# A two-layer attention kernel over graphs: tile loads of a turn spread over its slots, and q's last projection moved ahead of two value products

## The chip, the cores and the metric

The kernel runs on one core of one Trainium2 chip. The metric is the device time of one execution in microseconds (us), the median of the runs shown. One more execution was profiled, and the rows below are from it.

## What is computed

64 graphs of 256 nodes with 512 features each, and one adjacency matrix (256 x 256) that all graphs share. Two layers, both with a residual and a layer norm ahead:

```
h = max(layernorm(x), 0)
x = x + attention(h, adj; Wq, bq, Wk, bk, Wv, bv)        # 8 heads of 64, masked softmax
h = max(layernorm(x), 0)
rel = adj.T * (q @ k.T) ;  rel = rel / norm(rel, axis=2) # q = h Wq.T, k = h Wk.T
x = x + rel @ v                                          # v = h Wv.T
```

## The kernel before

**Precision.** Every operand of a large product is held as two fp16 halves, a high one (the fp16 rounding) and a low one (what is left). A product takes three matmuls for each part of the contraction (high x high, high x low, low x high: `SPLIT`). So one projection tile is 12 matmuls of 128 x 512 (`product`, L684).

**Unit of work.** Two graphs form a pair: 512 tokens, 4 tiles of 128. There are 32 pairs. For one pair TensorE makes, in layer 0, the projections `q`, `k`, `v` (4 tiles each), 4 groups of scores into the banks S, and 16 products `pv` (two graphs by eight heads) into the bank O; and in layer 1 the products `rv` and `rq` (4 each), `rel` (2) and `out` (4). Layer 1's q and k weights are multiplied once at the start (`setup_rq` makes `wm`), its v weight is transposed (`setup_rv` makes `wvt`). The products other than scores and pv take turns over three PSUM banks `B`; `free_bank` (L696) makes each wait until the one three places earlier has been evacuated. ACT writes the high half, DVE the low half.

**Transpositions.** What a product needs with the other axis on the partitions is turned by a DMA transposition from SBUF to SBUF, issued by SP: the softmax weights (`probs_t` from `halves`, L319, one for each of the 16 units of a pair), the normed input of layer 0 (`h0t`) and of layer 1 (`h1t`, L292, four each), and `rel_t` (L335, two). For a unit the chain is: scores on TensorE, mask and maximum on DVE (L620), exp on ACT (L481), high half on ACT (L489), low half on POOL (L375), transposition by SP (L319), `pv` on TensorE. The step `split` n stands for ACT's high half, POOL's low half and SP's transposition of unit n.

**Order.** Each engine runs a written-out order of steps. TensorE's is `TENSOR_PLAN`; `PLAN` is shared by SP, POOL, ACT and DVE, which each take the steps that they have a part in. A turn has 26 slots, one large product in each (`SLOTS`, with the number of pairs that the product lags behind); in a turn layer 0 of one pair runs beside layer 1 of the pair before, and out's products are those of two pairs before. `other_slot` puts the steps of a slot in order, and `LOADS` hangs the loads of x behind them: `x_in` (for the layer norm of a pair two turns ahead) and `x_res` (for the residual), four tiles of 128 x 512 fp32 each for a pair, issued by SP (L309, L316) in the same queue as the transpositions and the stores of the result (L340). In `LOADS` they stand two to a slot: x_in in slots 1 and 2, x_res in slots 13 and 14.

```
SLOTS = [("v", 0, 0), ("q", 0, 0), ("rel", 1, 2), ...
         ("k", 2, 0), ("rv", 0, 1), ("rv", 1, 1), ("q", 3, 0), ("rv", 2, 1), ...
LOADS = {13: [("x_res", 0, 0), ("x_res", 1, 0)], 14: [("x_res", 2, 0), ("x_res", 3, 0)],
         1: [("x_in", 0, -1), ("x_in", 1, -1)], 2: [("x_in", 2, -1), ("x_in", 3, -1)]}
```

Waits that matter here: `x_res` n of a pair waits until out n of the pair two before is written (L315); the first `residual` on POOL waits for all four x_res tiles (L388); `x_in` n waits until the tile before it in the buffer has been normed (L308); `rv` n waits for the transposition `h1t` n (L791), `pv` n for that of split n (L771). The buffers `halves` and `probs_t` are rings of four.

Of the kernel before, what the change touches and what calls it, by code (L numbers as in the profile page):

```python
# [5 lines left out]
def adjacency_attention_two_layers(  # L6
# [43 lines left out]

    SLOTS = [("v", 0, 0), ("q", 0, 0), ("rel", 1, 2), ("k", 0, 0), ("v", 1, 0), ("v", 2, 0), ("out", 0, 2),
# [11 lines left out]
    BESIDE = {1: [("squares", 0, 2), ("rel_scale", 0, 2)],
              2: [("residual", 2, 1), ("rel_split", 0, 2)],
              4: [("squares", 1, 2), ("rel_scale", 1, 2)],
              5: [("rel_split", 1, 2)],
              8: [("residual", 3, 1)],
# [7 lines left out]
              17: [("residual", 0, 0)],  # L75
              18: [("ln0_apply", 0, -1), ("ln0_split", 0, -1), ("ln0_apply", 1, -1), ("ln0_split", 1, -1)],
              21: [("ln0_apply", 2, -1), ("ln0_split", 2, -1)],
              23: [("residual", 1, 0)],
              24: [("ln0_apply", 3, -1), ("ln0_split", 3, -1)]}
# [3 lines left out]
    def on(at, steps):

        return [(kind, n, slot // PERIOD) for slot, kind, n in steps if slot % PERIOD == at]

    FIRST = [(slot, 2 * j) for j, slot in enumerate(MASKED)]
    SECOND = [(slot + 1, 2 * j + 1) for j, slot in enumerate(MASKED)]
    BY_UNIT = sorted(FIRST + SECOND)
    ENDED = [slot + 1 for slot in MASKED[1::2]]  # L90

    def tensor_slot(at):

        return (on(at, [(slot, "scores", m) for m, slot in enumerate(SCORED)]) + [SLOTS[at]]
                + on(at, [(slot, "pv", n) for n, slot in enumerate(MULTIPLIED)]))

    def other_slot(at):

        steps = on(at, [(slot + 1, "norm", m) for m, slot in enumerate(MULTIPLIED[3::4])])
        kind, n, back = SLOTS[at - 1]  # L100
        before = [(kind, n, back + (at == 0))]
        if kind == "v":
            steps += before
        steps += on(at, [(slot, "mask", n) for slot, n in FIRST])
        if kind != "v":
            steps += before
        steps += on(at, [(slot - 1, "mask", n) for slot, n in SECOND])
        steps += on(at, [(slot + 1, "inverse", m) for m, slot in enumerate(ENDED)])
        steps += BESIDE.get(at, [])
        for slot, n in BY_UNIT:  # L110
            steps += on(at, [(slot, "exp", n), (slot, "split", n)])
        return steps + LOADS.get(at, [])

    TENSOR_PLAN = [step for at in range(PERIOD) for step in tensor_slot(at)]
    PLAN = [step for at in range(PERIOD) for step in other_slot(at)]
    TURNS = PAIRS + 2

    PROJECT = [(kind, n) for kind, n, _ in SLOTS if kind in ("q", "k", "v")]
    RELATE = [(kind, n) for back in (1, 2) for kind, n, b in SLOTS if b == back]
# [7 lines left out]
    def pairs(plan):  # L127

        for turn in range(TURNS):
            for kind, n, back in plan:  # L130
                if kind in ("rv", "rq", "rel") and turn - back == -1 and (kind, n) in SETUP:
                    yield "setup_" + kind, n, turn - back
                elif 0 <= turn - back < PAIRS:
                    yield kind, n, turn - back
# [15 lines left out]
    with ctx:  # L150
# [18 lines left out]
        mask = sb("mask", [P, NT, N])  # L169
# [3 lines left out]
        x_in = sb("x_in", [P, TILES, D])  # L173
# [74 lines left out]
        residual = sem("residual")  # L248
# [8 lines left out]
        rel_scale = sem("rel_scale")  # L257
# [28 lines left out]
        def _(sp):  # L286
# [59 lines left out]
        def _(pool):  # L346
# [53 lines left out]
        def _(act):  # L400
# [56 lines left out]

            for kind, n, p in pairs(PLAN):
                if kind in ("q", "k"):
# [5 lines left out]
                    dst, b = (q_st, bq) if kind == "q" else (k_st, bk)  # L465
# [7 lines left out]
                elif kind == "exp":  # L473
                    m, g, e = unit(n)
# [51 lines left out]
        def _(dve):  # L526
# [72 lines left out]

            for kind, n, p in pairs(PLAN):  # L600
                if kind in ("q", "k"):
                    c = PROJECT.index((kind, n))
                    dve.wait_ge(p_high, NPC * p + c + 1)
                    dst, b = (q_st, bq) if kind == "q" else (k_st, bk)
# [9 lines left out]
                elif kind == "mask":  # L614
# [68 lines left out]
        def _(pe):  # L683
# [46 lines left out]

            for kind, n, p in pairs(TENSOR_PLAN):
                if kind in ("q", "k", "v"):
# [30 lines left out]
                elif kind == "pv":  # L763
                    m, g, e = unit(n)
# [16 lines left out]
                elif kind in ("rq", "rv", "rel", "out"):  # L781
# [18 lines left out]
                    else:  # L800
                        g, i = n // NT, n % NT
# [31 lines left out]
```

## Time and profile before

| | us |
|---|---|
| runs shown, median (lowest to highest) of 3 | 2463.25 (2459.55 to 2465.02) |
| the profiled execution's own time | 2464.18 |
| its span on the core | 2462.4 |
| TensorE busy | 2396.4 (97%) |
| ACT busy | 1686.4 (68%) |
| DVE busy | 1450.8 (59%) |
| POOL busy | 1298.9 (53%) |

Busy time of TensorE is the time in which a matmul is drawn, and a matmul is drawn somewhat longer than until the next can start. The chain that ended last is TensorE for 84% of the span, and the rest is spread over the other engines and the DMAs with at most 4% each. The DMA engines are busy for 64% of the span, nearly all of it with the packets of SP's queue.

### The profile page before, as it was taken

The page shows a single profiled execution, that of the slowest core. Times are in us where ns is not written, and L with a number is a line of the kernel's source. Part 1 is how long each engine was busy: PE and PEld are TensorE (multiplying, and loading weights), DVE is VectorE, ACT ScalarE, POOL GpSimd, SP SyncE. Part 2 cuts the span into 40 slices and gives each one's busy share as a digit, 9 for nine tenths or more (in the row PEclk, how much of TensorE's full clock was granted, in tenths as well). Part 3 has the DMA queues.
Part 4 walks back from the last instruction along what each step waited for, and adds up shares of the span by engine and source line. Part 5 has one row for each costly group of instructions (what it writes and reads, how often), then busy time and mean ns, then how long its engine had stood idle before and what let it go on. Part 6 is the DMA issues. An engine that isn't in the chain of part 4 may idle for free.

```text
span 2462.4 us, 53549 instructions
## 1 busy us (share of the span) xinstructions
PE 2396.4 (97%) x19252; PEld 1301.3 (53%) x19252; DVE 1450.8 (59%) x4435; ACT 1686.4 (68%) x4111; POOL 1298.9 (53%) x1159
## 2 busy tenths in 40 slices
PE   6999999999999999999999999999999999999986
PEld 3455555555555555555555555555555555555543
DVE  5555666555666556666555665555665556666543
ACT  5667777667676677776677766776776776766762
POOL 3555555555555555555555555555555555555541
PEclk9999999999999999999999999999999999999998
DMA  7566666676676566666665766665755666765652
GB/s 207 111 133 135 131 147 138 123 140 130 137 148 129 120 137 129 153 138 130 126 138 129 151 133 126 140 138 126 150 138 123 140 135 132 150 136 120 124 111 65
DMA packets 938841, 329.14 MB, mean 134 GB/s; under 512 B 885968, under 2 KB 886224, under 8 KB 938576
## 3 DMA queue, kind: packets, MB, share of 16 engines
q1 hardware_dynamic: 935744, 322.31, 63.1%
q8 instruction: 153, 2.51, 0.5%
q10 hardware_dynamic: 2832, 3.41, 0.4%
q14 instruction: 112, 0.92, 0.1%
HBM read 73.93 MB, written 33.55 MB: 44 GB/s over the span
## 4 chain that ended last, share of the span: by engine, by line
PE 84%; DMA 4%; DVE 4%; ACT 3%; POOL 3%; issue 2%; SPq 1%; ACTq 0%; DVEq 0%
PE B L686 70%; PE S L759 7%; PE O L686 6%; DMA probs_t<-halves 3%; ACT probs L481 1%; DVE stats L545 1%; POOL halves L375 1%; ACT h L421 1%; POOL v L371 1%; DMA h1t<-h_halves 1%; PE B L716 1%; ACT halves L489 0%; POOL h_halves L361 0%; ACT h_halves L428 0%; DVE masked L620 0%
## 5 line engine op out<-in xcount | busy, mean ns | idle before, releaser
L375 POOL TENSOR_TENSOR halves<-probs,halves 128x512 f16<-128x512 f32 x512 | 596.5, 1167 | 532.8 <-ACT halves L489 532.6
L481 ACT ACTIVATE probs<-masked,neg_max 128x256 f32<-128x256 f32 x1024 | 508.4, 498 | 222.5 <-DVE neg_max L620 221.8
L620 DVE CUSTOM_DVE_ANT_0 masked<-S,mask 128x256 f32<-128x256 f32 x1024 | 386.4, 417 | 129.4 <-PE S L759 129.3
L361 POOL TENSOR_TENSOR h_halves<-h,h_halves 128x512 f16<-128x512 f32 x256 | 295.0, 1158 | 150.4 <-ACT h_halves L428 150.4
L686 PE MATMUL B<-wv,h0t 128*128 128x512 f16 x1536 | 355.0, 381 | 19.4 <-DMA h0t<-h_halves 19.4
L686 PE MATMUL B<-wvt,h1t 128*128 128x512 f16 x1536 | 349.5, 381 | 12.6 <-DMA h1t<-h_halves 12.6
L686 PE MATMUL B<-h0t,wq 128*128 128x512 f16 x1536 | 352.8, 379 | 1.0 <-DVE k_st L605 0.5
L686 PE MATMUL B<-h0t,wk 128*128 128x512 f16 x1536 | 352.5, 379 | 0.0
L686 PE MATMUL B<-h1t,wm 128*128 128x512 f16 x1536 | 346.9, 379 | 0.0
L489 ACT ACTIVATE halves<-probs 128x512 f16<-128x512 f32 x512 | 322.5, 630 | 16.2
L686 PEld LDWEIGHTS O<-v,probs_t 128*128 128x128 f16 x6144 | 247.7, 98 | 143.0 <-DMA probs_t<-halves 23.8
L686 PE MATMUL O<-v,probs_t 128*128 128x64 f16 x6144 | 263.3, 193 | 17.6 <-DMA probs_t<-halves 17.6
L371 POOL TENSOR_TENSOR v<-v_sum,v 128x512 f16<-128x512 f32 x128 | 148.4, 1159 | 180.9 <-ACT v L472 180.8
L686 PEld LDWEIGHTS B<-wvt,h1t 128*128 128x128 f16 x1536 | 142.0, 98 | 182.8 <-issue 22.6
L391 POOL TENSOR_TENSOR x_res<-x_res,attn 128x512 f32<-128x512 f32 x128 | 162.5, 1269 | 143.7 <-DMA x_res<-in_x_dram 120.8
L686 PEld LDWEIGHTS B<-h0t,wq 128*128 128x128 f16 x1536 | 145.4, 98 | 174.6 <-issue 6.8
L686 PEld LDWEIGHTS B<-wv,h0t 128*128 128x128 f16 x1536 | 141.7, 98 | 179.3 <-issue 28.9
L686 PEld LDWEIGHTS B<-h1t,wm 128*128 128x128 f16 x1536 | 146.1, 98 | 166.6
L686 PEld LDWEIGHTS B<-h0t,wk 128*128 128x128 f16 x1536 | 145.8, 98 | 159.5
L472 ACT ACTIVATE v<-v_sum 128x512 f16<-128x512 f32 x128 | 80.6, 630 | 203.9 <-DVE v_sum L612 203.9
L686 PE MATMUL B<-rv,rel_t 128*128 128x512 f16 x768 | 189.9, 385 | 6.4 <-issue 5.7
L759 PE MATMUL S<-k_st,q_st 64*128 64x256 f16 x3072 | 189.9, 270 | 4.3 <-DVE k_st L605 4.3
(70 smaller groups left out, 2941.8 us busy)
## 6 DMA issues: line engine op xcount, KB each, us to landing
x_in<-in_x_dram SPq DMA_DIRECT2D x128, 256.0 KB, 3.2
x_res<-in_x_dram SPq DMA_DIRECT2D x128, 256.0 KB, 3.8
out_dram<-result SPq DMA_DIRECT2D x128, 256.0 KB, 2.5
probs_t<-halves SPq DMA_TRANSPOSE x512, 2.9
h0t<-h_halves SPq DMA_TRANSPOSE x128, 3.2
h1t<-h_halves SPq DMA_TRANSPOSE x128, 3.3
rv<-in_L_gnn_Wv_dram ACTq DMA_DIRECT2D x2, 512.0 KB, 6.0
rq<-in_L_gnn_Wq_dram ACTq DMA_DIRECT2D x2, 512.0 KB, 7.6
```

Of the source, the lines that this page charges most:

```text
L361: nc.gpsimd.tensor_tensor(h_halves[:, n, 1, :], h[:, n % 2, :], h_halves[:, n, 0, :], ALU.subtract).then_inc(h_low[layer], 1)
L371: nc.gpsimd.tensor_tensor(v[:, p % 2, 1, n, :], v_sum[:, n % 2, :], v[:, p % 2, 0, n, :], ALU.subtract).then_inc(v_low, 1)
L375: nc.gpsimd.tensor_tensor(halves[:, n % RING, 1, :], probs[:, n % 2, :, :].rearrange("p t n -> p (t n)"), halves[:, n % RING, 0, :], ALU.s ...
L391: nc.gpsimd.tensor_tensor(cols, cols, attn[:, n % 2, :, :].rearrange("p (t e) d -> p t (e d)", e=2), ALU.add).then_inc(residual, 1)
L421: nc.scalar.activation(h[:, n % 2, :], src[:, n, :], ACT.Relu, scale=rstd[:, layer, n:n + 1], bias=shift[:, layer, n:n + 1]).then_inc(ln_d ...
L472: nc.scalar.activation(v[:, p % 2, 0, n, :], v_sum[:, n % 2, :], ACT.Copy).then_inc(p_high, 1)
L481: ins = nc.scalar.activation(probs[:, n % 2, i, :], masked[:, n % 2, i, :], ACT.Exp, bias=neg_max[:, n % 2, i:i + 1], scale=-1.0, accum_ou ...
L489: nc.scalar.activation(halves[:, n % RING, 0, :], probs[:, n % 2, :, :].rearrange("p t n -> p (t n)"), ACT.Copy).then_inc(halved_high, 1)
L545: ins = nc.vector.bn_stats(stats[:, layer, t, :], src[:, t, :])
L620: ins = nc.vector.tensor_tensor_reduce(out=masked[:, n % 2, i, :], in0=S[n % 4][:, i, :], in1=mask[:, i, :], scale=SCORE, scalar=BIG, op0= ...
L686: ins = nc.tensor.matmul(dst, left(i), right(j), start=(n == 0), stop=(n == len(pairs) - 1))
L759: ins = nc.tensor.matmul(S[2 * g + e][:, i, :], q_st[own, n, hq, col(g * NT + i)], k_st[own, n, hk, col(g, N)], start=(t == 0), stop=(t == ...
```

## The change

The slots of a turn and the lists of steps are replaced by a table that gives each step of a pair a slot counted from the pair's own start, and a place within the slot; `in_order` sorts the steps of all pairs by slot, place and pair. For TensorE this gives the old order but for one product: q 3 stands at slot 15 and rv 0 and rv 1 at 16 and 17, where before rv 0 and rv 1 stood at 15 and 16 and q 3 at 17. The steps of ACT and DVE that evacuate them move along. The loads of x have slots of their own: x_in at slots 1, 3, 4 and 6 of a turn, x_res at 8, 10, 14 and 15. POOL's order stays as it is. Nothing is added or left out. The code of the engines changes in the name of the list only.

```diff
-    SLOTS = [("v", 0, 0), ("q", 0, 0), ("rel", 1, 2), ("k", 0, 0), ("v", 1, 0), ("v", 2, 0), ("out", 0, 2),
...
+    PRODUCT_AT = {("v", 0): 0, ("q", 0): 1, ("k", 0): 3, ("v", 1): 4, ("v", 2): 5, ("v", 3): 7, ("q", 1): 9,
+                  ("k", 1): 10, ("q", 2): 13, ("k", 2): 14, ("q", 3): 15, ("k", 3): 24,
+                  ("rv", 0): 42, ("rv", 1): 43, ("rv", 2): 44, ("rv", 3): 45, ("rq", 0): 46, ("rq", 1): 47,
...
-    LOADS = {13: [("x_res", 0, 0), ("x_res", 1, 0)], 14: [("x_res", 2, 0), ("x_res", 3, 0)],
-             1: [("x_in", 0, -1), ("x_in", 1, -1)], 2: [("x_in", 2, -1), ("x_in", 3, -1)]}
+    LAYER0 = {"x_in": [-25, -23, -22, -20], "ln0_stats": [-14, -14, -13, -13], "ln0_power": [-13],
+              "ln0_scale": [-10], "ln0_apply": [-8, -8, -5, -2], "ln0_split": [-8, -8, -5, -2],
+              "x_res": [8, 10, 14, 15], "residual": [17, 23, 28, 34]}
...
+    def timetable():
+
+        tensor = [(slot, 0, "scores", m) for m, slot in enumerate(SCORED)]
+        tensor += [(slot, 1, kind, n) for (kind, n), slot in PRODUCT_AT.items()]
+        tensor += [(slot, 2, "pv", n) for n, slot in enumerate(MULTIPLIED)]
...
+        for j, slot in enumerate(MASKED):
+            others += [(slot, 2, "mask", 2 * j), (slot, 4, "mask", 2 * j + 1)]
+            others += [(slot + e, 7, kind, 2 * j + e) for e in range(2) for kind in ("exp", "split")]
+        for layer in (LAYER0, LAYER1):
+            for n in range(TILES):
+                others += [(at[n], 8 if kind[0] == "x" else 6, kind, n) for kind, at in layer.items() if n < len(at)]
+        return tensor, others
+
+    def in_order(steps):
+
+        order = []
+        for p in range(-1, PAIRS):
+            for i, (slot, place, kind, n) in enumerate(steps):
+                if p >= 0 and not (p == 0 and slot < 0):
+                    order.append((PERIOD * p + slot, place, p, i, kind, n))
+                elif p < 0 and (kind, n) in SETUP:
+                    order.append((PERIOD * p + slot, place, p, i, "setup_" + kind, n))
+        return [(kind, n, p) for _, _, p, _, kind, n in sorted(order)]
...
+    TENSOR_PLAN, PLAN = [in_order(steps) for steps in timetable()]
...
-            for kind, n, p in pairs(PLAN):
+            for kind, n, p in PLAN:
```

TensorE, a turn in the middle, from the second group of scores on. `B<-h0t,wq` is a tile of q, `B<-h0t,wk` of k, `B<-wvt,h1t` of rv, `O<-v,probs_t` one pv. Before:

```order
L759 MATMUL S<-k_st,q_st 128x256 x24
L686 MATMUL B<-h0t,wq 128x512 x12
L686 MATMUL O<-v,probs_t 128x64 x12
L686 MATMUL B<-h0t,wk 128x512 x12
L686 MATMUL O<-v,probs_t 128x64 x12
L686 MATMUL B<-wvt,h1t 128x512 x24
L686 MATMUL B<-h0t,wq 128x512 x12
L686 MATMUL O<-v,probs_t 128x64 x12
L686 MATMUL B<-wvt,h1t 128x512 x12
```

And with the change:

```order
L729 MATMUL S<-k_st,q_st 128x256 x24
L656 MATMUL B<-h0t,wq 128x512 x12
L656 MATMUL O<-v,probs_t 128x64 x12
L656 MATMUL B<-h0t,wk 128x512 x12
L656 MATMUL O<-v,probs_t 128x64 x12
L656 MATMUL B<-h0t,wq 128x512 x12
L656 MATMUL B<-wvt,h1t 128x512 x24
L656 MATMUL O<-v,probs_t 128x64 x12
L656 MATMUL B<-wvt,h1t 128x512 x12
```

q 3 has moved ahead of rv 0 and rv 1; the pv behind them is pv 4 in both. (The changed file is 30 lines shorter ahead of the engines' code, so its line numbers are 30 less.)

SP's queue in a turn in the middle, from the h1t transpositions to split 7 (`halves` into `probs_t`: splits 4, 5, 6 and 7). Before:

```order
L292 DMA_TRANSPOSE h1t<-h_halves 128x8x128 x4
L340 DMA out_dram<-result 128x512
L319 DMA_TRANSPOSE probs_t<-halves 128x8x128
L316 DMA x_res<-in_x_dram 128x512 x2
L319 DMA_TRANSPOSE probs_t<-halves 128x8x128
L316 DMA x_res<-in_x_dram 128x512 x2
L319 DMA_TRANSPOSE probs_t<-halves 128x8x128 x2
```

With the change, from the second x_res load on:

```order
L286 DMA x_res<-in_x_dram 128x512
L310 DMA out_dram<-result 128x512
L262 DMA_TRANSPOSE h1t<-h_halves 128x8x128 x4
L310 DMA out_dram<-result 128x512
L289 DMA_TRANSPOSE probs_t<-halves 128x8x128 x2
L286 DMA x_res<-in_x_dram 128x512 x2
L289 DMA_TRANSPOSE probs_t<-halves 128x8x128 x2
```

x_res 0 and 1 no longer stand between splits 4 and 5, and x_res 1 stands ahead of the store of out 2 and of h1t; x_res 2 and 3 are still side by side, right behind split 5.

SP's queue around splits 14 and 15 of a pair and 0 of the next. Before:

```order
L309 DMA x_in<-in_x_dram 128x512 x2
L335 DMA_TRANSPOSE rel_t<-rel_halves 128x8x128
L319 DMA_TRANSPOSE probs_t<-halves 128x8x128
L309 DMA x_in<-in_x_dram 128x512 x2
L319 DMA_TRANSPOSE probs_t<-halves 128x8x128
L335 DMA_TRANSPOSE rel_t<-rel_halves 128x8x128
L319 DMA_TRANSPOSE probs_t<-halves 128x8x128
L340 DMA out_dram<-result 128x512
```

With the change, down to the first x_res load:

```order
L279 DMA x_in<-in_x_dram 128x512
L305 DMA_TRANSPOSE rel_t<-rel_halves 128x8x128
L289 DMA_TRANSPOSE probs_t<-halves 128x8x128 x2
L279 DMA x_in<-in_x_dram 128x512 x2
L305 DMA_TRANSPOSE rel_t<-rel_halves 128x8x128
L289 DMA_TRANSPOSE probs_t<-halves 128x8x128
L279 DMA x_in<-in_x_dram 128x512
L310 DMA out_dram<-result 128x512
L289 DMA_TRANSPOSE probs_t<-halves 128x8x128
L286 DMA x_res<-in_x_dram 128x512
```

Splits 14 and 15 now stand together with one load ahead of them instead of two and two; x_in 3 has moved behind split 0 of the next pair, and x_res 0 of that pair behind its split 1.

## Rows read from the trace of the kernel before

**Rows 1.** Stretch 138 to 2365: length, TensorE busy, granted clock, DMA share, GB/s.
```profile
138.00:2365.00 2227.00, 2215.99 (x17969) 1.00 0.66 135
```

**Rows 2.** TensorE's waits from 130 to 2350: total us, times, longest.
```profile
PE O L686 <- DMA probs_t<-halves: 8.9, 11, 2.1
PE B L686 <- DMA h1t<-h_halves: 2.1, 2, 1.3
```

**Rows 3.** Timeline, first S group of turns 2, 30 and 31: start, length.
```profile
171.57 1.48 PE L759 MATMUL S<-k_st,q_st 64*128 64x256 f16 x24
...
2255.03 1.48 PE L759 MATMUL S<-k_st,q_st 64*128 64x256 f16 x24
...
2328.96 1.48 PE L759 MATMUL S<-k_st,q_st 64*128 64x256 f16 x24
```

**Rows 4.** Timeline, TensorE waits before pv 5, rv 0, pv 15, pv 5, pv 14.
```profile
503.21 0.52 PE L686 MATMUL O<-v,probs_t 128*128 128x64 f16 x12 [1.17 <-DMA probs_t<-halves]
...
715.85 4.48 PE L686 MATMUL B<-wvt,h1t 128*128 128x512 f16 x20 [1.32 <-DMA h1t<-h_halves]
...
846.22 0.52 PE L686 MATMUL O<-v,probs_t 128*128 128x64 f16 x12 [1.77 <-DMA probs_t<-halves]
...
1175.94 0.52 PE L686 MATMUL O<-v,probs_t 128*128 128x64 f16 x12 [2.08 <-DMA probs_t<-halves]
...
1439.27 0.52 PE L686 MATMUL O<-v,probs_t 128*128 128x64 f16 x12 [0.49 <-DMA probs_t<-halves]
```

**Rows 5.** Timeline of turn 13, h1t to pv 5; SPq is SP issuing.
```profile
1011.52 6.13 SPq L292 DMA_TRANSPOSE h1t<-h_halves  x4
...
1014.92 5.34 PE L686 MATMUL B<-wvt,h1t 128*128 128x512 f16 x24
...
1018.32 1.31 SPq L319 DMA_TRANSPOSE probs_t<-halves  x1
1018.33 1.16 POOL L375 TENSOR_TENSOR halves<-probs,halves 128x512 f16<-128x512 f32 x1 [0.61 <-ACT halves L489]
...
1019.68 1.05 SPq L316 DMA_DIRECT2D x_res<-in_x_dram  x2
...
1020.10 2.75 PE L686 MATMUL B<-h0t,wq 128*128 128x512 f16 x12
...
1020.77 1.24 SPq L319 DMA_TRANSPOSE probs_t<-halves  x1
...
1022.05 1.06 SPq L316 DMA_DIRECT2D x_res<-in_x_dram  x2
...
1025.63 0.51 PE L686 MATMUL O<-v,probs_t 128*128 128x64 f16 x12
```

**Rows 6.** The page, DMA issues: count, median us from issue to landing.
```profile
probs_t<-halves SPq DMA_TRANSPOSE x512, 2.9
...
h1t<-h_halves SPq DMA_TRANSPOSE x128, 3.3
```

**Rows 7.** Landing, split 5 in turns 0, 13, 15, 31; last row: split 4, turn 13.
```profile
DMA to landing us min/median/max: 3.7/3.7/3.7
...
DMA to landing us min/median/max: 3.9/3.9/3.9
...
DMA to landing us min/median/max: 7.4/7.4/7.4
...
DMA to landing us min/median/max: 3.8/3.8/3.8
...
DMA to landing us min/median/max: 2.8/2.8/2.8
```

**Rows 8.** Timeline of the start: q 3 and pv 5 of turn 0, rv 0 of turn 1.
```profile
55.33 2.76 PE L686 MATMUL B<-h0t,wq 128*128 128x512 f16 x12 [0.54 <-DVE k_st L605]
...
59.76 0.52 PE L686 MATMUL O<-v,probs_t 128*128 128x64 f16 x12 [0.85 <-DMA probs_t<-halves]
...
119.57 0.81 PE L686 MATMUL B<-wvt,h1t 128*128 128x512 f16 x3 [0.98 <-DMA h1t<-h_halves]
```

More of the change, by code:

```diff
@@ L48, in adjacency_attention_two_layers @@
     RING = 4
-    SLOTS = [("v", 0, 0), ("q", 0, 0), ("rel", 1, 2), ("k", 0, 0), ("v", 1, 0), ("v", 2, 0), ("out", 0, 2),
[3 rows of a table removed]
-    PERIOD = len(SLOTS)
+    PERIOD = 26
+    PRODUCT_AT = {("v", 0): 0, ("q", 0): 1, ("k", 0): 3, ("v", 1): 4, ("v", 2): 5, ("v", 3): 7, ("q", 1): 9,
[3 rows of a table added]
+                  ("out", 0): 58, ("out", 1): 60, ("out", 2): 63, ("out", 3): 64}
+    PROJECT = [(kind, n) for kind, n in PRODUCT_AT if kind in ("q", "k", "v")]
+    RELATE = [(kind, n) for kind, n in PRODUCT_AT if kind in ("rv", "rq", "rel", "out")]
     SCORED = [6, 13, 19, 26]
@@ L61, in adjacency_attention_two_layers @@
     MULTIPLIED = [10, 11, 13, 14, 17, 18, 20, 21, 23, 24, 26, 27, 29, 30, 31, 32]
[L63 to L67, printed above, removed]
[7 rows of a table removed]
[L75 to L79, printed above, removed]
@@ L80, in adjacency_attention_two_layers @@
-    LOADS = {13: [("x_res", 0, 0), ("x_res", 1, 0)], 14: [("x_res", 2, 0), ("x_res", 3, 0)],
-             1: [("x_in", 0, -1), ("x_in", 1, -1)], 2: [("x_in", 2, -1), ("x_in", 3, -1)]}
[L83 to L119, printed above, removed]
+    LAYER0 = {"x_in": [-25, -23, -22, -20], "ln0_stats": [-14, -14, -13, -13], "ln0_power": [-13],
+              "ln0_scale": [-10], "ln0_apply": [-8, -8, -5, -2], "ln0_split": [-8, -8, -5, -2],
+              "x_res": [8, 10, 14, 15], "residual": [17, 23, 28, 34]}
@@ new lines, in adjacency_attention_two_layers @@
+    LAYER1 = {"ln1_stats": [35, 35, 36, 36], "ln1_power": [36], "ln1_scale": [38], "ln1_apply": [38] * TILES,
+              "ln1_split": [38] * TILES, "squares": [53, 56], "rel_scale": [53, 56], "rel_split": [54, 57]}
+    def timetable():
+        tensor = [(slot, 0, "scores", m) for m, slot in enumerate(SCORED)]
+        tensor += [(slot, 1, kind, n) for (kind, n), slot in PRODUCT_AT.items()]
+        tensor += [(slot, 2, "pv", n) for n, slot in enumerate(MULTIPLIED)]
+        others = [(slot + 1, 0, "norm", m) for m, slot in enumerate(MULTIPLIED[3::4])]
+        others += [(slot + 1, 1 if kind == "v" else 3, kind, n) for (kind, n), slot in PRODUCT_AT.items()]
+        others += [(slot + 2, 5, "inverse", m) for m, slot in enumerate(MASKED[1::2])]
+        for j, slot in enumerate(MASKED):
[5 more added lines that the diff above has]
+        return tensor, others
@@ L125, in adjacency_attention_two_layers @@
     NSETUP = len(SETUP)
[L127 to L134, printed above, removed]
+    TENSOR_PLAN, PLAN = [in_order(steps) for steps in timetable()]
     KINDS = ("q", "k", "v", "rv", "rq", "rel", "out", "setup_rv", "setup_rq", "setup_rel")
-    PRODUCTS = [step for step in pairs(TENSOR_PLAN) if step[0] in KINDS]
+    PRODUCTS = [step for step in TENSOR_PLAN if step[0] in KINDS]
     BANKS = 3
@@ L366, in _ @@
                 h_low_half(0, n, 0)
-            for kind, n, p in pairs(PLAN):
+            for kind, n, p in PLAN:
                 if kind == "v":
@@ L456, in setup_high_half @@
                     nc.scalar.activation(dst, bank_[:, :], ACT.Copy, scale=WS).then_inc(setup_high, 1)
-            for kind, n, p in pairs(PLAN):
+            for kind, n, p in PLAN:
                 if kind in ("q", "k"):
@@ L598, in setup_low_half @@
                                                    ALU.mult, ALU.subtract).then_inc(setup_done, 1)
-            for kind, n, p in pairs(PLAN):
+            for kind, n, p in PLAN:
                 if kind in ("q", "k"):
@@ L729, in setup_chunk @@
                 ins.then_inc(setup_product, 1)
-            for kind, n, p in pairs(TENSOR_PLAN):
+            for kind, n, p in TENSOR_PLAN:
                 if kind in ("q", "k", "v"):
```

11 rows, old and new, of tables (BESIDE, PRODUCT_AT, SLOTS) are left out of this document.

## The prediction

> **What bounds the kernel now.** I read the page's busy times first, and TensorE alone is near the span (2396.4 of 2462.4 us). Between 138 and 2365 us it is busy 2215.99 of 2227.00 us at a granted clock of 1.00 (the 2.4 GHz level) [rows 1]. Only TensorE's waits can pay in that stretch, and they are few: 13 shown waits, 11.0 us in all, every one on the landing of a DMA transposition, `probs_t` (11) or `h1t` (2) [rows 2].
>
> To see what lies beyond the shown waits I took the start of the first S group of a turn [rows 3]. From turn 30 to 31 it is 73.93 us, the shortest distance and that of a dozen turns. From turn 2 to 31 it is 2157.39 us for 29 turns, where 29 x 73.93 would be 2143.97: **13.4 us are lost**. The shown waits of these turns make 10.5 (0.54 of the 11.0 fall just ahead of turn 2). The rest is hidden by the modelled ends: a group of 24 is drawn until 1020.26 while the next starts at 1020.10 [rows 5], so each wait is drawn 0.16 us too short (12 x 0.16 = 1.9). 1.0 us is left in waits too short to show. TensorE's own work stays, so this pot and a few waits of the start are all that the change can win.
>
> Where do the 13 waits stand? Before pv 5 (between rv 2 and scores 2): four, 4.5 us, 2.08 and 1.17 the longest. Before pv 15 (between out 0 and v 3): three, 2.6 us, the longest 1.77. Before pv 14: four, 1.9 us, one of 0.49 shown. Before rv 0: two, 2.1 us, the longest 1.32 [rows 4]. These are exactly the places that the change touches.
>
> Then the queue on SP in a turn without a long wait, turn 13 [rows 5]. POOL ends the low half of split 5 at 18.33 + 1.16 = 1019.49. Its transposition is issued at 1020.77, after split 4's own issue (1018.32 to 1019.63) and the two x_res loads (1019.68, two in 1.05 us). It lands 3.9 us later [rows 7], at 1024.67; pv 5 starts at 1025.63. So it has 0.96 us of slack. Transpositions in general land after 2.9 us, this one after 3.7 to 7.4: 3.7 in turn 0, 3.8 in turn 31, median 4.2 of its 32 [rows 6, 7]. The 7.4 is turn 15, and there pv 5 waits 2.08 us [rows 4]. Split 15 is alike: x_in 2 and 3 stand right ahead of it. rv 0 has another reason: the h1t transposition of tile 0 is issued at 1011.52 and lands after 3.3, at 1014.8, and rv 0 starts at 1014.92 [rows 5, 6]. It has 0.1 us of slack in every turn.
>
> **The change part by part.**
>
> *q 3 ahead of rv 0.* It adds no instruction. rv 0 moves back by one product: 1014.92 to 1020.10 are two, so 2.59 us [rows 5]. Its slack becomes 0.1 + 2.6 = 2.7 us, and the longest wait there, 1.32, is gone. I count the two waits (2.1 + 2 x 0.16 = 2.4) and 0.8 of the 1.0 us of small ones, since it is the only place with 0.1 us of slack: **-3.2**. What could be late instead: the bank. Banks go round by three, so the product at each place still waits for the one three places earlier, and that one is evacuated at the same place of ACT's and DVE's programs as before (q 3 now stands where rv 0 stood). rv 3 and rq 0, which now need the banks of rv 0 and rv 1, have a pv and a scores group between. Zero. The wait of q 3 before (k's scores of the pair before) is long past. Zero.
>
> *x_res 0 and 1 no longer between split 4 and split 5.* Split 5 is issued when split 4's issue ends, 1019.65, instead of 1020.77 here; over the turns the distance of 2.44 would mostly fall to 1.8, where POOL is ready, so 0.65 us sooner. And no load is ahead of it in its queue: landing 2.8 to 2.9 instead of 4.2, 1.3 us sooner. Slack 0.96 + 2.0 = 3.0 us. All four waits go: 4.5 + 4 x 0.16 = **-5.1**. The lower bound is the issue alone with the landing unchanged: of the 2.08 then 1.4 stay, of the 1.17 still 0.5, and with the hidden parts about 2.5 of the 5.1 are won.
>
> *x_in 2 and 3 no longer between split 14 and split 15.* The same by 1.1 us of issue (two loads' worth, as the 1.05 us above) and about 1 of landing. The three waits: 2.6 + 3 x 0.16 = **-3.1**; lower bound 2 (1.77 less 1.1 stays).
>
> *x_in 1 no longer ahead of rel's transposition and split 14.* One load of 256 KB less in the queue, the issue of split 14 is unchanged since rel's transposition waits for DVE. Between nothing and all of 1.9 + 4 x 0.16 = 2.5; I take the middle, **-1.25**, as no row decides.
>
> *The start.* q 3 of turn 0 waited 0.54 us for k 2's bank, since two short setup groups stood between; in the new order it needs k 1's bank, long free, and the setup group that needs k 2's comes 2.6 us later. pv 5 of turn 0 waited 0.85 behind the same x_res pair, rv 0 of the first turn 0.98 [rows 8]. With 3 x 0.16: **-2.85**. Lower bound 1.
>
> *What it costs.* Three single loads now stand ahead of other transpositions: x_in 3 ahead of split 1, x_res 0 ahead of split 2, x_res 1 ahead of h1t. By the timeline these land 3.2, 5.9 and (with q 3 moved) 2.7 us before they are needed, and one load costs 0.6 us of issue. x_in 1 and 2 stand ahead of the second rel transposition, which has some 8 us. No wait is added: x_res n needs only out n of two turns earlier, which stands ahead of it on SP. POOL is idle until the x_res loads land in each turn, and they are issued 1 us sooner, which only helps pv 7. I put down **+1.0** for landings that are late by chance at the new places; ends 0 and 3.
>
> Sum: -3.2 - 5.1 - 3.1 - 1.25 - 2.85 + 1.0 = -14.5. The profiled execution took 2464.18 us (span 2462.4), 0.9 above the median of the three runs, 2463.25. 2464.18 - 14.5 = 2449.7; I forecast **2449.5**, as what is won are mostly waits that vary from run to run (2459.55 to 2465.02) and what is left hardly does.
>
> **A rule weighed.** Split 4's transposition has the x_res pair right behind it and lands after 2.8 us in turn 13 as in the median turn; split 5's, with a pair ahead and a pair behind, after 3.9 [rows 5, 7]. I read this as: what is ahead costs, what is behind doesn't. The Trainium skill, "DMA: Bandwidth & Descriptors", section on queues, rings and completion order, says that a later descriptor may finish its write before an earlier one, and that completion is not first in, first out for one issuing engine. By it a pair behind could hurt as well, and in the changed kernel x_res 2 and 3 still stand right behind split 5. The sum would be that of the first rival, 2453.
>
> **The rivals.**
> 1. *Loads behind a transposition hurt as much.* Then pv 5 and pv 15 win the issue time alone (2.5 of 5.1, 2 of 3.1): 2449.5 + 3.7 = 2453.2. For it: the 7.4 of turn 15 has loads on both sides. Against: split 4. Chance 0.15.
> 2. *Late landings are chance and fall elsewhere.* Half of the waits before pv 5 and pv 15 stay (4.1) and all before pv 14 (1.25): 2449.5 + 5.4 = 2454.9. For it: landings of 4.4 to 5.0 us occur here and there at nearly every place of a turn. Against: landings over 5.5 us are found in steady turns only beside load pairs. Chance 0.15.
> 3. *The transposition isn't what is late, the low half ahead of it is*, so moving loads does nothing, or the change doesn't do what it says: x_res 2 and 3 and x_in 1 and 2 are still pairs on SP. Only rv 0 (3.2) and its first wait (1.1) are won: 2459.9, no change. Against: split 5's low half is ready 1.28 us before its issue. Chance 0.09.
> 4. *Slower: h1t behind x_res 1.* x_res 1 now goes out just before out 2's store and the four h1t transpositions. Its place is rv 0, in all 31 turns; the slack there is 2.7 over a landing of 3.3, so it begins to cost at 6.0 us and eats the whole gain at 6.0 + 14.5/31 = 6.5. At 7.4 us each turn [rows 7] it costs 1.4 x 31 = 43: 2493. For it: 7.4 was seen with two loads around. Against: it is one load, issued 2 us before h1t is ready. Chance 0.03.
>
> **How the numbers follow.** The forecast has 0.58. A measurement of this kernel can tell 0.2% from no change, 4.9 us, so faster means below 2458.3. Forecast and rivals 1 and 2 lie there: 0.88 faster; rival 3: 0.09 same; rival 4: 0.03 slower. The range: below, all of the pot with nothing new and half more from pv 14, 2446.5; above, rival 2 with two more microseconds of chance, 2457.5. Outside are rivals 3 and 4 and a little of the rest.
>
> **What the changed profile would show.** A turn of 73.9 us nearly everywhere (over 73.93 by less than 0.15 on average, now 0.46); shown steady waits of some 2 us instead of 11; none before rv 0 except in the last turn (9.5 us there, where no q 3 exists); split 5 issued 1.8 us after split 4 and landing after 2.8. The waits of the last turn, after 2390 us, unchanged. It would be wrong if split 5 still landed after 4 us or more, if waits for `h1t` grew, or if waits appeared before pv 1 or pv 2.

## The result, and the profile after

| | before | changed |
|---|---|---|
| median of 6 runs (lowest to highest), us | 2462.39 (2459.55 to 2465.02) | 2453.95 (2452.83 to 2455.27) |
| the profiled execution's own time | 2464.18 | 2453.71 |
| its span | 2462.4 | 2451.9 |
| start of the first S group of turn 0 | 35.36 | 35.17 |
| turn 0 / turn 1 | 62.25 / 73.96 | 63.90 / 73.47 |
| turns 2 to 30, over 29 x 73.93 | 13.4 | 2.1 |
| from the first S group of turn 31 to the end | 133.4 | 133.3 |

The ratio is 0.996, with a 95% interval from 0.995 to 0.997: the kernel became faster, by 8.4 us of the medians and 10.5 us of the profiled executions. The time lies inside the range that was stated, 4.5 us above the forecast. The table says where the two differ from the plan: the turns in the middle gave 11.4 us, where 11.65 were forecast, and turn 0, which was to give time too, took 1.65 us more.

The page of the changed kernel, busy times, and the windows view of its middle (length, TensorE busy, granted clock, DMA share, GB/s):

```profile
PE 2395.6 (98%) x19252; PEld 1302.3 (53%) x19252; DVE 1442.2 (59%) x4435; ACT 1686.0 (69%) x4111; POOL 1300.1 (53%) x1159
```

```profile
138.00:2355.00 2217.00, 2215.78 (x17988) 1.00 0.66 136
```

Where 11.0 us were idle in 2227 [rows 1], it is now 1.2 in 2217. TensorE's waits from 130 to 2340 us of the changed kernel, the answer to [rows 2]:

```profile
PE O L656 <- DMA probs_t<-halves: 1.0, 4, 0.5
PE B L656 <- DVE q_st L575: 0.2, 1, 0.2
```

No wait for `h1t` is left, and none stands before pv 5 or pv 15. The four for `probs_t` stand before pv 14 (three) and pv 1 (one). The first S groups of turns 2, 30 and 31, the answer to [rows 3]:

```profile
172.54 1.48 PE L729 MATMUL S<-k_st,q_st 64*128 64x256 f16 x24
...
2244.64 1.48 PE L729 MATMUL S<-k_st,q_st 64*128 64x256 f16 x24
...
2318.57 1.48 PE L729 MATMUL S<-k_st,q_st 64*128 64x256 f16 x24
```

A clean turn is 73.93 us as before; 2318.57 - 172.54 = 2146.03 is 2.06 over 29 of them. The timeline of turn 13, from h1t to split 5, the answer to [rows 5]:

```profile
1006.91 5.85 SPq L262 DMA_TRANSPOSE h1t<-h_halves  x4
...
1010.25 2.75 PE L656 MATMUL B<-h0t,wq 128*128 128x512 f16 x12
...
1012.84 5.35 PE L656 MATMUL B<-wvt,h1t 128*128 128x512 f16 x24
1013.43 2.70 SPq L289 DMA_TRANSPOSE probs_t<-halves  x2
1013.72 1.16 POOL L345 TENSOR_TENSOR halves<-probs,halves 128x512 f16<-128x512 f32 x1 [0.61 <-ACT halves L459]
```

q 3 starts where rv 0 started, and rv 0 2.59 us later. Splits 4 and 5 go out one behind the other. Split 5 is issued at 1014.90, as POOL ends its low half, and lands after

```profile
DMA to landing us min/median/max: 2.8/2.8/2.8
```

that is at 1017.7, 3.3 us before pv 5 (1020.97), where it had 0.96. Over all turns from 2 on split 5 is issued 1.7 us after split 4 instead of 2.44.

And the start, TensorE from 56 to 64 us, which answers to the first two of [rows 8]:

```profile
56.11 1.04 PE L692 MATMUL B<-ident,rv 128*128 128x128 f32 x8
...
57.84 0.66 PE L692 MATMUL B<-ident,rv 128*128 128x128 f32 x4 [0.34 <-DVE q_st L575]
58.33 0.51 PE L656 MATMUL O<-v,probs_t 128*128 128x64 f16 x12
58.77 1.48 PE L729 MATMUL S<-k_st,q_st 64*128 64x256 f16 x24
62.88 0.66 PE L692 MATMUL B<-ident,rv 128*128 128x128 f32 x4 [2.62 <-DVE wvt L567]
```

pv 5 of turn 0 no longer waits, but setup_rv 3 now waits 2.62 us until DVE has evacuated the bank of setup_rv 0. In the kernel before it didn't wait.

### The profile page after: what moved, and what is told of

Same layout as the page of the kernel before. It is cut to its first block, busy times and chain, and to the rows that moved or that the text cites. A ratio compares the mean times of both kernels' runs of the same rounds, so it can differ in the third digit from the quotient of the medians.

```text
span 2451.9 us, 53549 instructions
## 1 busy us (share of the span) xinstructions
PE 2395.6 (98%) x19252; PEld 1302.3 (53%) x19252; DVE 1442.2 (59%) x4435; ACT 1686.0 (69%) x4111; POOL 1300.1 (53%) x1159
## 3 DMA queue, kind: packets, MB, share of 16 engines
HBM read 73.93 MB, written 33.55 MB: 44 GB/s over the span
## 4 chain that ended last, share of the span: by engine, by line
PE 93%; DVE 2%; ACT 2%; DMA 1%; issue 1%; POOL 1%; ACTq 0%; DVEq 0%; SPq 0%
PE B L656 78%; PE S L729 7%; PE O L656 7%; DMA probs_t<-halves 1%; ACT probs L451 1%; PE B L686 1%; DVE stats L515 0%; ACT h L391 0%; ACT halves L459 0%; POOL v L341 0%; DVE masked L590 0%; POOL halves L345 0%; ACT h_halves L398 0%; ACTq L377 0%; POOL sq_pow L366 0%
```

## The experiments

They ran on three chips, and the kernel before took a different time on each (medians 2470.07, 2464.29 and 2466.41 us; 2462.39 above). Kernels of one chip are compared with each other, and turns and landings are read from each kernel's profiled execution. The waits by place are taken from the starts of TensorE's rows in turns 2 to 30 (what a step's distance from the one ahead is over its usual distance), hidden parts included:

| turns 2 to 30, us over the usual distance | rv 0 | pv 5 | pv 14 | pv 15 | pv 1 | sum | turn 0, us |
|---|---|---|---|---|---|---|---|
| before | 2.9 | 5.4 | 1.9 | 3.2 | - | 13.4 | 62.25 |
| changed | 0.3 | - | 1.4 | - | 0.5 | 2.1 | 63.90 |
| q 3 alone | - | 5.4 | 1.8 | 4.8 | - | 12.1 | 62.46 |
| loads alone | 9.8 | - | 2.7 | - | 1.4 | 14.1 | 61.52 |
| changed, start as before | 0.4 | - | 2.1 | - | 1.4 | 3.9 | 61.52 |
| before, narrow x_res loads | 2.2 | - | 1.4 | 6.8 | - | 10.2 | 62.40 |

### q 3 alone

```diff
-             ("k", 2, 0), ("rv", 0, 1), ("rv", 1, 1), ("q", 3, 0), ("rv", 2, 1), ("rv", 3, 1), ("rq", 0, 1),
+             ("k", 2, 0), ("q", 3, 0), ("rv", 0, 1), ("rv", 1, 1), ("rv", 2, 1), ("rv", 3, 1), ("rq", 0, 1),
```

> The kernel before with q 3 ahead of rv 0 and rv 1 alone; the loads stay in pairs. My theory: in turns 2 to 31 the waits before rv 0 go (3.2 us), those before pv 5, pv 14 and pv 15 stay (8 to 10 us), and turn 0 loses 2.6 us to a wait of setup_rv 3 for the bank of setup_rv 0, less what pv 5 and q 3 of turn 0 gave up: the turn is 1 to 2 us longer than before. Together 2 to 3 us less than before, ratio 0.999. Rival (the start's loss comes from the loads): turn 0 is not longer, 4 us less.

Measured: 2468.43 us against 2470.07, ratio 0.9993 (0.9984 to 1.0002): no difference that can be told. TensorE's waits from 130 to 2345 us:

```profile
PE O L686 <- DMA probs_t<-halves: 9.0, 13, 2.4
```

The waits for h1t are gone and those for probs_t are all there, as expected. Turn 0 is 0.2 us longer, not 1 to 2: the 2.6 us wait did not come, so it is not q 3's move alone that makes it. Whether the loads alone make it, the next run answers.

### The loads alone

```diff
-                  ("k", 1): 10, ("q", 2): 13, ("k", 2): 14, ("q", 3): 15, ("k", 3): 24,
-                  ("rv", 0): 42, ("rv", 1): 43, ("rv", 2): 44, ("rv", 3): 45, ("rq", 0): 46, ("rq", 1): 47,
+                  ("k", 1): 10, ("q", 2): 13, ("k", 2): 14, ("q", 3): 17, ("k", 3): 24,
+                  ("rv", 0): 41, ("rv", 1): 42, ("rv", 2): 44, ("rv", 3): 45, ("rq", 0): 46, ("rq", 1): 47,
```

> The changed kernel with q 3 back behind rv 1 and rv 0 and rv 1 one slot earlier: the loads' new slots alone. My theory: 8 to 9 us won in turns 2 to 31 (split 5 lands after 2.9 us and is issued 1.8 after split 4), the waits before rv 0 come back (about 3 us in turns 2 to 31), turn 0 keeps the 62 us of before or less, no wait of setup_rv 3: 9 us less than before, ratio 0.996, the same total as the changed kernel by another way. Rival (late landings are chance): the waits before pv 5 and pv 15 are found again in part, 5 us less.

Measured: 2463.38 against 2470.07, ratio 0.9974 (0.9965 to 0.9983): faster by 6.7 us. The execution that was profiled (2465.21) is the slowest of the ten. TensorE's waits from 130 to 2350 us:

```profile
PE B L656 <- DMA h1t<-h_halves: 6.4, 6, 1.6
PE O L656 <- DMA probs_t<-halves: 3.1, 6, 0.9
```

The loads did what was expected at pv 5 and pv 15, but the waits before rv 0 did not come back at 3 us: they are 9.8, in 20 of the 29 turns (2.9 in the kernel before, 2.2 in the kernel with narrow loads, on this chip). x_res 1 now stands ahead of the h1t transpositions, and the one of tile 0 lands after 3.4 us at the median instead of 3.2, with five over 4 instead of two. Where rv 0 has 0.1 us of slack, each of these is a wait. With x_res 1 behind split 5 instead (the run with four loads there) the landing is 3.2 again. So **the two halves of the change help each other**: the new place of x_res 1 costs some 7 us at rv 0 in this execution, and q 3 ahead of it gives the 2.6 us that hide this. By the medians of this chip the loads give 6.7 us, q 3 gives 1.6, and both together (the next kernel) 16.0. Turn 0 is 61.52: the loads alone don't make its wait either.

### The changed kernel with the start as before

```diff
             for i, (slot, place, kind, n) in enumerate(steps):
+                if p == 0 and (kind, n) == ("q", 3):
+                    slot += 2
+                if p < 0 and (kind, n) in (("rv", 0), ("rv", 1)):
+                    slot -= 1
```

> The changed kernel, but in turn 0 q 3 behind the first two setup groups as before. My theory: the 2.6 us wait of setup_rv 3 goes, turn 0 takes about 61.5 us instead of 63.9, all else as in the changed kernel: 2 to 3 us less than the changed kernel, ratio 0.9955 to before. Rival: the time is only moved to the next wait for a landing in turn 0, nothing won.

Measured: 2454.05 against 2470.07, ratio 0.9937 (0.9925 to 0.9949). Turn 0 takes 61.52 us, 2.38 less than in the changed kernel, and the wait is gone. The middle lost 3.9 us in this execution and 2.1 in that of the changed kernel, and the stretch from turn 31 on took 1.2 us more, so the two spans are the same (2452.5 and 2451.9): what the middle loses differs by some 2 us from one execution to the next. On this one chip the step from the loads alone to this kernel, which is q 3's move from turn 1 on, is 9.3 us (2463.38 to 2454.05), where q 3 alone gave 1.6 that can't be told from nothing.

### The kernel before with narrow x_res loads

```diff
-                    sp.dma_start(x_res[:, p % 2, n, :], xv[p][:, n, :]).then_inc(res_loaded[p % 2], 16)
+                    c = D if p < 2 else 16
+                    sp.dma_start(x_res[:, p % 2, n, :c], xv[p][:, n, :c]).then_inc(res_loaded[p % 2], 16)
```

> The kernel before, order untouched, but from pair 2 on each x_res load brings 16 of the 512 columns (so the residual of these pairs is added to what lies there). It takes the bytes ahead of and behind split 5 away and leaves the issues. If the bytes in the queue make split 5 late, it lands after 2.8 to 2.9 us at an unchanged 2.44 us behind split 4, and no wait stands before pv 5 after turn 2: 4 to 5 us less. If the issues are the cause, its landing and the waits before pv 5 stay. The waits before pv 15 and rv 0 stay in both cases.

The kernel leaves out 496 of the 512 columns of each x_res tile from pair 2 on.

Measured: 2464.27 against 2470.07, ratio 0.9977 (0.9967 to 0.9988). SP's queue from 1015 to 1020 us has the same issues, 2.44 us from split 4 to split 5, as before:

```profile
1015.28 1.31 SPq L320 DMA_TRANSPOSE probs_t<-halves  x1
1016.63 1.05 SPq L317 DMA_DIRECT2D x_res<-in_x_dram  x2
1017.72 1.24 SPq L320 DMA_TRANSPOSE probs_t<-halves  x1
1019.00 1.04 SPq L317 DMA_DIRECT2D x_res<-in_x_dram  x2
```

But split 5 lands after 2.8 us at the median (4.2 before), and no wait is left before pv 5. The bytes in the queue made it late, the issues did not (ahead of it or behind, this run doesn't tell; the one with four loads behind does). pv 15, beside the untouched x_in pair, kept its waits (6.8 us in this execution).

### The changed kernel again, on the second chip

> The changed kernel once more, on the chip of the next three, so that they can be set against it. Turns 2 to 31 lose 2 to 4 us, turn 0 takes 63.9 us with a wait of 2.6 for setup_rv 0's bank; three small instructions of DVE's layer norm scale (L507, L509, L534) take 1.1 to 1.2 us each in turn 0, each until a POOL instruction ends.

Measured: 2455.80 against 2464.29, ratio 0.9959 (0.9944 to 0.9974); turn 0 63.90, the middle 2.6 over. The three instructions took 1.13, 1.18 and 1.07 us. In the first profile of the changed kernel they are these, and with them comes the answer to the lost start (DVE and POOL, timeline from 55 to 66 us):

```profile
58.57 0.16 DVE L505 TENSOR_TENSOR ln_work<-ln_work,guess 128x4 f32<-128x4 f32 x1
58.71 1.16 POOL L345 TENSOR_TENSOR halves<-probs,halves 128x512 f16<-128x512 f32 x1 [4.51 <-ACT halves L459]
58.77 1.13 DVE L507 TENSOR_SCALAR ln_work<-ln_work 128x4 f32<-128x4 f32 x1
59.83 1.27 POOL L361 TENSOR_TENSOR x_res<-x_res,attn 128x512 f32<-128x512 f32 x1
59.93 1.19 DVE L509 TENSOR_TENSOR rstd<-guess,ln_work 128x4 f32<-128x4 f32 x1
61.05 1.16 POOL L345 TENSOR_TENSOR halves<-probs,halves 128x512 f16<-128x512 f32 x1
61.15 1.07 DVE L534 SCALAR_TENSOR_TENSOR shift<-moments,rstd 128x4 f32<-128x4 f32 x1
62.15 1.27 DVE L567 SCALAR_TENSOR_TENSOR wvt<-B,wvt 128x512 f16<-128x512 f32 x2
```

One of these instructions on 128 x 4 elements takes 0.16 us when POOL is idle and 1.1 to 1.2 when it is not: each of the three ends as the POOL instruction beside it ends (59.87, 61.10, 62.21). The low half of setup_rv 0 (L567) stands behind them, and TensorE waits for it. The same rows with q 3 alone, where the x_res loads are late and POOL has a gap:

```profile
58.73 1.12 DVE L537 TENSOR_SCALAR ln_work<-ln_work 128x4 f32<-128x4 f32 x1
59.88 0.16 DVE L539 TENSOR_TENSOR rstd<-guess,ln_work 128x4 f32<-128x4 f32 x1
60.08 0.16 DVE L564 SCALAR_TENSOR_TENSOR shift<-moments,rstd 128x4 f32<-128x4 f32 x1
60.16 0.68 DVE L597 SCALAR_TENSOR_TENSOR wvt<-B,wvt 128x512 f16<-128x512 f32 x1
```

Two of the three are short, and the low half starts 2.0 us sooner. The Trainium skill, "SBUF — State Buffer", says that VectorE and GpSimd share a port pair of SBUF under an exclusive lock, that whichever starts first holds it for its whole instruction, and that a VectorE instruction with two SBUF inputs or in a 2-port mode has to wait for it. The rows agree for L509 and L534, which read two tiles in SBUF: 1.19 and 1.07 us. L507 reads one tile and was held too, 1.13 us; whether it ran in a 2-port mode no row shows. In the next kernel a low half (L567), which reads a PSUM bank and one tile in SBUF, took its usual 0.69 us beside POOL (59.51, with POOL busy from 59.07 to 60.24).

### The layer norm's scale one slot later

```diff
-              "ln0_scale": [-10], "ln0_apply": [-8, -8, -5, -2], "ln0_split": [-8, -8, -5, -2],
+              "ln0_scale": [-9], "ln0_apply": [-8, -8, -5, -2], "ln0_split": [-8, -8, -5, -2],
```

> The changed kernel with DVE's layer norm scale of layer 0 one slot later, behind the low half of rv 0 (of setup_rv 0 in turn 0) instead of ahead of it. My theory: what keeps setup_rv 0's bank in turn 0 is that its evacuation stands behind five small DVE instructions, three of which are held until POOL's instruction ends, since the x_res tiles now come sooner and POOL works without a gap. With the scale behind it the bank is free 3 us sooner, the 2.6 us wait goes and turn 0 takes about 61.3 us: 2.4 us less than the changed kernel. The layer norm's apply on ACT comes up to 1 us later, which its 14 us of slack take. Rival (the bank is late because ACT's high half is late): the wait of setup_rv 3 stays above 1.5 us.

Measured: 2454.53 against 2464.29, ratio 0.9957 (0.9943 to 0.9972), not to be told from the changed kernel (2455.80). Turn 0 is 63.72. The wait of setup_rv 3 went, and the next evacuation took its place: setup_rv 1's low half is now the one behind the scale, and setup_rq 0 waits for that bank (TensorE's timeline of this kernel, from 40 to 80 us):

```profile
63.64 3.70 PE L686 MATMUL B<-x_res,rq 128*128 128x512 f32 x8 [2.44 <-DVE wvt L567]
```

My expectation was wrong in the size (2.4 us less were expected, 0.2 came); its rival was not right either, for ACT's high half was in time.

### POOL's residual two slots later

```diff
-              "x_res": [8, 10, 14, 15], "residual": [17, 23, 28, 34]}
+              "x_res": [8, 10, 14, 15], "residual": [19, 23, 28, 34]}
```

> The changed kernel with POOL's first residual step two slots later, behind split 7 and the first two low halves of the layer norm. My theory: in turn 0 the small DVE instructions of the scale are slow because POOL works without a gap behind split 6; with the residual moved POOL idles for some 0.9 us between split 6 and split 7, so L509 takes 0.16 us instead of 1.19 and L534 is done 1 us or more sooner, and the wait of 2.6 us for setup_rv 0's bank shrinks to 1 to 1.6: turn 0 takes 62.3 to 62.9 us instead of 63.9. Rival (these instructions are slow for another reason, such as a first use): they take 1.1 us each as before and turn 0 stays at 63.9.

Measured on the third chip: 2454.07 against 2466.41, ratio 0.9950 (0.9935 to 0.9965). The changed kernel was not run on this chip, so it is turn 0 that answers: 62.45 us, inside what was expected. Neither DVE nor TensorE was touched, only POOL has a gap behind split 6:

```profile
59.12 1.15 POOL L345 TENSOR_TENSOR halves<-probs,halves 128x512 f16<-128x512 f32 x1 [4.54 <-ACT halves L459]
59.17 1.12 DVE L507 TENSOR_SCALAR ln_work<-ln_work 128x4 f32<-128x4 f32 x1
60.33 0.16 DVE L509 TENSOR_TENSOR rstd<-guess,ln_work 128x4 f32<-128x4 f32 x1
60.53 0.16 DVE L534 SCALAR_TENSOR_TENSOR shift<-moments,rstd 128x4 f32<-128x4 f32 x1
60.61 0.68 DVE L567 SCALAR_TENSOR_TENSOR wvt<-B,wvt 128x512 f16<-128x512 f32 x1
61.24 1.16 POOL L345 TENSOR_TENSOR halves<-probs,halves 128x512 f16<-128x512 f32 x1 [0.97 <-ACT halves L459]
61.34 0.42 PEld L692 LDWEIGHTS B<-ident,rv 128*128 128x128 f32 x4 [0.96 <-DVE wvt L567]
61.34 0.66 PE L692 MATMUL B<-ident,rv 128*128 128x128 f32 x4 [0.69 <-DVE wvt L567]
```

The two instructions are short again and the wait shrank from 2.62 to 0.69 us (0.43 more came before setup_rq 0). So two instructions held by POOL make 1.45 of the 2.4 us that turn 0 takes less with the start as before. The first of the three is still held (1.12 us), and waits of 0.69 and 0.43 us stay with it; that they are its price was not tried by itself.

### All four x_res loads behind split 5

```diff
-              "x_res": [8, 10, 14, 15], "residual": [17, 23, 28, 34]}
+              "x_res": [14, 14, 14, 14], "residual": [17, 23, 28, 34]}
```

> The changed kernel with all four x_res loads in slot 14, right behind split 5 and ahead of split 6. If only what stands ahead of a transposition costs, split 5 still lands after 2.9 us at the median and 4 at the most, and split 6, with four loads ahead, after 5 or more, which its 6 us of slack cover; no wait before pv 5, and as much time as the changed kernel within 1 us (rv 0 loses nothing, as x_res 1 no longer stands ahead of h1t). If what stands behind costs too, split 5 lands after 4 or more and waits before pv 5 are found again: 2 to 5 us more than the changed kernel.

Measured: 2454.76 against 2466.41, ratio 0.9956 (0.9939 to 0.9973), not to be told from the kernel ahead. SP's queue from 1011 to 1018 us, and the landings of split 5 and split 6 there:

```profile
1011.31 2.65 SPq L289 DMA_TRANSPOSE probs_t<-halves  x2
1014.01 2.00 SPq L286 DMA_DIRECT2D x_res<-in_x_dram  x4
1016.21 1.29 SPq L289 DMA_TRANSPOSE probs_t<-halves  x1
```

```profile
DMA to landing us min/median/max: 2.9/2.9/2.9
...
DMA to landing us min/median/max: 4.4/4.4/4.4
```

With four loads (1 MB) right behind it split 5 lands after 2.9 us at the median and 4.0 at the most, as with two behind it in the changed kernel (2.9 and 3.9); with four ahead split 6 needs 5.1. What stands behind a transposition costs it nothing that these rows show. Turn 0 takes 62.46 us, as in the kernel ahead, and without a change of POOL's order: the x_res loads are late, POOL waits 1.27 us for them, and L509 and L534 take 0.16 us each.

Not every load ahead costs either. In the changed kernel two x_res loads stand right ahead of split 6, as they did ahead of split 5 before. But split 6 waits for POOL and goes out 1.5 us after them, and it lands after 3.1 us at the median, where split 5 had 4.2 (SP's queue from 1016 to 1020 us of the changed kernel):

```profile
1016.18 1.05 SPq L286 DMA_DIRECT2D x_res<-in_x_dram  x2
1018.76 1.24 SPq L289 DMA_TRANSPOSE probs_t<-halves  x1
```

What the landings follow is how long the last load or store ahead still needs when the transposition is issued. Over the `probs_t` transpositions of turns 2 to 30 in five profiled executions (before, changed, this one and the two with other x_in places) the medians are:

| the last one ahead lands ... us after the issue | the transposition lands after, us |
|---|---|
| 1.5 to 2.0 | 2.8 to 2.9 |
| 2.0 to 2.5 | 3.2 to 3.4 |
| 2.5 to 3.0 | 3.6 to 4.1 |
| 3.0 to 3.5 | 4.2 |
| 3.5 to 4.5 | 4.5 to 5.0 |

From 2 us on that is 0.9 to 1.2 us behind the one ahead. The 7.4 us of turn 15 fit: the load ahead of split 5 took 7.0 us itself, and split 5 landed 0.94 us behind it. No run set this distance by itself.

### x_in 3 beside x_in 2

```diff
-    LAYER0 = {"x_in": [-25, -23, -22, -20], "ln0_stats": [-14, -14, -13, -13], "ln0_power": [-13],
+    LAYER0 = {"x_in": [-25, -23, -22, -22], "ln0_stats": [-14, -14, -13, -13], "ln0_power": [-13],
```

> The changed kernel with x_in 3 in the slot of x_in 2, so that only the store of out 0 stands ahead of split 1, as before the change. If one load together with the store makes split 1 land after 4.1 us instead of 2.9, it lands after 2.9 again and no wait stands before pv 1 in turns 2 to 31; three loads in a row stand ahead of the second rel transposition, which has 8 us. 0.5 to 1 us less than the changed kernel, too little to measure but to be seen in the landings. Rival (the landing of split 1 is late through the turn's new phase): it stays above 3.8.

Measured: 2453.35 against 2464.29, ratio 0.9953 (0.9938 to 0.9967), 2.4 us under the changed kernel of the same chip with ranges that overlap; the middle of its profiled execution lost 2.4 us against 2.6, so the difference of the medians is not shown to be this move's. The landings answer it: split 1 after 2.9 us at the median (none of 32 over 4) instead of 4.1 (20 over 4), and no wait before pv 1. One load together with a store ahead of a transposition costs it 1.2 us, where the store alone costs nothing.

### The x_in loads where there is slack

```diff
-    LAYER0 = {"x_in": [-25, -23, -22, -20], "ln0_stats": [-14, -14, -13, -13], "ln0_power": [-13],
+    LAYER0 = {"x_in": [-33, -32, -30, -28], "ln0_stats": [-14, -14, -13, -13], "ln0_power": [-13],
```

beside the edit of the start as before.

> Turn 0's order as in the run with the start as before, and the four x_in loads moved to slots 19, 20, 22 and 24 of the turn, behind splits 8, 9, 10 and h1t's counterpart of layer 0, where the next pv's have 6 to 8 us of slack. The thinnest place left, pv 14 (1.4 us of slack), then has no x_in load within 10 us ahead. My theory: splits 14, 15, 1 land after 2.9 at the median; turns 2 to 31 lose 1 us instead of 2 to 4; turn 0 61.5 us. 4 us less than the changed kernel. Rival: what holds split 14 now and then is not the loads (4.4 to 5.0 us landings are found everywhere), pv 14 keeps 1 to 2 us of waits: 3 us less.

Measured: **2451.96 us (2451.20 to 2452.00)** against 2464.29, ratio 0.9945 (0.9931 to 0.9960), and 2455.80 (2453.41 to 2456.71) for the changed kernel on the same chip: 3.8 us less than the change, with ranges that don't touch. TensorE's waits from 130 to 2340 us are one:

```profile
PE O L660 <- DMA probs_t<-halves: 0.2, 1, 0.2
```

The middle is 0.3 us over 29 clean turns, so in this execution the pot of the steady turns is empty. Turn 0 takes 61.51, 2.4 less than in the changed kernel, and turn 1 takes 74.59, 1.1 more. That pv 14 lost 0.4 us only is no proof of the theory: with the x_in loads in the changed kernel's places it lost 0.5 in the run with four loads behind split 5 and 2.4 in the one ahead of that. Splits 9 and 11, which now have a single load ahead, land after 3.6 and 3.2 us instead of 2.9 and 2.7 and can afford it. This version beats both kernels.

## Why the prediction was right or wrong

**The bound and the pot: right.** 13.4 us were read as lost in the turns from 2 on, and 11.4 of them came back; a turn is 73.93 us in all kernels.

**q 3 ahead of rv 0: right in the changed kernel, wrong as a price.** The term was 3.2 us; by the starts of the rows 2.9 stood there, and 0.3 is left. That rest is not a landing: its shown part is the wait for DVE's q_st among TensorE's waits above, a bank, for which nothing was put down. Slack of 2.5 us at the median appears where 2.7 was forecast (2.1 in turn 13: h1t lands 3.8 after 1006.91, rv 0 starts at 1012.84). But the term leaned on a landing that the other half of the change made worse. Without q 3's move rv 0 waited 9.8 us. Rival 4 had the mechanism and the right place, and with the slack of 2.7 it named the reason why it doesn't show.

**x_res, x_in 2 and 3: right.** No wait is left before pv 5 and pv 15. Split 5 was to be issued 1.8 us after split 4 and land after 2.8: 1.7 and 2.9. Narrow loads and four loads behind it show together that the bytes ahead are what costs; the reading lacked that they cost only as far as they are still under way (the table above). Rival 1 falls, as loads behind cost nothing. Rival 2 falls at these places: split 5 never lands after more than 4 us (18 of 32 before), and split 15 in 5 turns instead of 14, which its 3.3 us of slack now cover.

**x_in 1 and pv 14: put down too high, and no gain is shown.** The term was 1.25 us, the middle of a range. 1.9 became 1.4, and the landings did not change: split 14 lands after 3.2 us at the median before and 3.1 after, and over 4 us in 7 of 32 turns in both. In the other kernels with x_in 1 moved pv 14 lost from 0.4 to 2.7 us, in those with it in its old place 1.8 and 1.4. The middle still came out near its sum, since pv 5 gave 0.3 more than forecast and the cost was smaller.

**What it costs: right in size.** +1.0 was put down; split 1 is late now (4.1 us), and pv 1 lost 0.5 us in the changed kernel and 1.1 in its second profile. A wait before pv 1 was named as a sign of being wrong; it came, but no larger than the term.

**The start: wrong, and this is the step that failed.** It was to give 2.85 us (with turn 1). Turn 1 gave 0.5 and turn 0 took 1.65, so the first two turns, with the 0.2 us that the first S group starts sooner, cost 1.0 instead: 3.8 us of the gap. Two sentences carried it. "rv 3 and rq 0, which now need the banks of rv 0 and rv 1, have a pv and a scores group between. Zero." holds where a product is 2.6 us, but in turn 0 these products are setup groups of 0.5 us. And "POOL is idle until the x_res loads land in each turn, and they are issued 1 us sooner, which only helps pv 7" took POOL's idle time for worthless: it was the time in which DVE's small instructions ran in 0.16 us. In the changed kernel POOL has no gap, two of them take 1 us more, and setup_rv 0's bank is late by that; with the gap back turn 0 takes 1.45 us less, and the rest of the 2.4 is not traced to one cause. Neither half does it alone (turn 0 62.46 and 61.52), as it takes q 3's move, which puts the low half behind the scale, and the early loads. That the time lies in the range all the same is luck: the upper end had 8 us of room for late landings, and the start, which was given no such room, used 3.8 of them.

**The rest of the gap** is in what is compared. The sum was made against an execution of 2464.18 us; the median of the six runs is 2462.39. 14.5 forecast, less 3.8 at the start and 0.3 in the middle, is 10.4, which is the difference of the profiled executions (10.5); less 1.8, as the profiled execution was slower than the median, and 0.2, as the changed kernel's was faster, it is 8.4. Which waits are missing in a middling run of the kernel before is not shown, as one execution of it was profiled.

## What to carry to other kernels

A DMA transposition on the critical chain pays for the loads ahead of it in its queue that are still under way when it is issued, and not for those behind. So a load goes right behind the transposition that is wanted soon, and ahead of one that has slack or is issued some time later. Work out the slack of each transposition (its landing to the start of its reader) before moving a load: one table of these shows both the waits and where the loads can go. And an idle stretch on one engine may be what another runs in; an engine that gets its input sooner can slow its neighbour.

## What was unexpected of the hardware

- Instructions of DVE on 128 x 4 elements took 0.16 us beside an idle POOL and up to 1.19 us beside a POOL instruction of 1.16 to 1.27, ending with it each time.
- The landing of one transposition (2.8 us alone) took 2.8 or 2.9 with a 256 KB store right ahead, 3.2 or 3.6 with one 256 KB load, 4.1 with a load and a store, 4.2 with two loads and 5.1 with four, but 3.1 with two loads that were issued 1.5 us sooner, and 2.9 with four behind.
- The same kernel before took 2462.4, 2464.3, 2466.4 and 2470.1 us (medians) in four sessions, while the changed kernel and its variants with both halves stayed between 2452.0 and 2455.8. What the chips differ in is not shown. No execution of the kernel before was profiled on those three chips, and late landings are not more frequent in the variants' traces from the slowest of them (36 of 512 `probs_t` transpositions over 4.4 us with the start as before, against 43 in the changed kernel's first profile and 29 in its second).
